# Attention scores of eight-wide heads in two 64-row tiles of TensorE, six bf16 products in place of nine, and their parts stored in stack order

## What is computed

```python
h = _layernorm(x) * (1 + ca) + sa
x = x + ga * attention_1(h)        # 16 heads of width 16, causal softmax
h = _layernorm(x) * (1 + cb) + sb
x = x + gb * ffn(h)
# ffn: layernorm, attention_2 (32 heads of width 8, full softmax), + input,
#      then per batch two of eight experts, 256 tokens each:
#      gelu(tokens @ w1 + b1) @ w2 + b2
```

## Time and profile before

| | us |
|---|---|
| median of three runs (1864.37 to 1867.82) | 1865.28 |
| span of the profiled execution | 1866.4 |
| TensorE matmuls busy | 1646.4 (88%) |
| VectorE busy | 1197.6 (64%) |
| ScalarE busy | 1020.4 (55%) |
| GpSimd busy | 479.6 (26%) |

### The profile page before, as it was taken

One profiled execution on the slowest core, in us unless ns is written; L12 is line 12 of the kernel. 1 busy time (PEld: TensorE's weight loads), 2 busy tenths in 40 slices (PEclk: granted clock), 3 DMA queues, 4 the chain that ended last, 5 costly groups with the idle time before them and its releaser, 6 DMA issues.

```text
span 1866.4 us, 32448 instructions
## 1 busy us (share of the span) xinstructions
PE 1646.4 (88%) x8721; PEld 717.9 (38%) x8721; DVE 1197.6 (64%) x3093; ACT 1020.4 (55%) x1967; POOL 479.6 (26%) x804
## 2 busy tenths in 40 slices
PE   3487769999899989999899989999899997989887
PEld 1223313336333543346333443335333452325325
DVE  7466367864787567864787557964687566665440
ACT  0044425765567555765467645765467654665561
POOL 7133312232232222331232221331231232200100
PEclk9789869999999999999899999999999999999898
DMA  4540162243443452243334342243324243132301
GB/s 113 124 96 20 55 134 62 61 93 82 114 92 81 84 130 55 61 99 81 103 81 95 78 130 62 69 94 87 103 72 95 73 100 72 35 63 68 97 2 57
DMA packets 92282, 152.61 MB, mean 82 GB/s; under 512 B 19748, under 2 KB 78180, under 8 KB 83820
## 3 DMA queue, kind: packets, MB, share of 16 engines
q1 hardware_dynamic: 92100, 150.40, 33.8%
HBM read 119.58 MB, written 29.59 MB: 80 GB/s over the span
## 4 chain that ended last, share of the span: by engine, by line
PE 67%; DVE 9%; DMA 7%; issue 6%; ACT 6%; SPq 3%; POOL 1%; DVEq 0%; POOLq 0%; ACTq 0%
PE bank_out L1058 14%; PE bank_scores L1042 13%; PE bank_max L1021 12%; PE bank_side L993 6%; PE bank_side L1148 5%; DMA q_stack<-max_parts 4%; PE bank_side L1006 3%; PE bank_misc L1132 3%; DVE neg_max L1250 3%; PE bank_side L1132 3%; ACT probs L855 2%; PE bank_side L1113 2%; SPq L646 2%; PE bank_misc L1067 2%; PE bank_misc L1103 1%
## 5 line engine op out<-in xcount | busy, mean ns | idle before, releaser
L855 ACT ACTIVATE probs<-bank_scores 128x512 f32<-128x512 f32 (+3 forms) x1536 | 790.4, 544 | 629.8 <-PE bank_scores L1042 624.9
L1250 DVE TENSOR_REDUCE neg_max<-bank_max 128x1 f32<-128x512 f32 x1024 | 668.7, 682 | 266.1 <-PE bank_max L1021 261.7
L1042 PE MATMUL bank_scores<-q_stack,k_stack 128*128 128x512 bf16 (+3 forms) x1536 | 555.2, 366 | 70.0 <-DMA q_stack<-max_parts 42.6
L1021 PE MATMUL bank_max<-k_stack,q_stack 125*128 125x512 bf16 (+3 forms) x1536 | 559.2, 372 | 58.7 <-issue 21.5
L1058 PE MATMUL bank_out<-probs,v_tile 128*9 128x512 f32 (+4 forms) x3072 | 367.6, 551 | 1.0 <-POOL probs L766 0.9
L1247 DVE CUSTOM_DVE_ANT_0 bank_max<-bank_max,causal 128x128 f32<-128x128 f32 (+3 forms) x512 | 247.4, 506 | 183.7 <-PE bank_max L1021 180.0
L1021 PEld LDWEIGHTS bank_max<-k_stack,q_stack 125*128 125x128 bf16 x1536 | 150.1, 99 | 441.3 <-issue 293.8
L1042 PEld LDWEIGHTS bank_scores<-q_stack,k_stack 128*128 128x128 bf16 x1536 | 151.4, 99 | 309.5 <-ACT probs L855 153.2
L748 POOL CAST max_parts<-max_row 16x128 bf16<-16x128 f32 x96 | 26.8, 279 | 593.7 <-DVE max_row L1261 593.4
L766 POOL TENSOR_SCALAR_AFFINE_SELECT probs<-probs 128x512 f32<-128x512 f32 x128 | 81.1, 634 | 343.4 <-ACT probs L855 343.4
L1148 PE MATMUL bank_side<-w_out,hidden_T 128*128 128x256 f32 x512 | 132.6, 386 | 13.7 <-ACT hidden_T L891 10.7
(11 more groups left out here) (115 smaller groups left out, 1388.1 us busy)
## 6 DMA issues: line engine op xcount, KB each, us to landing
q_stack<-q_parts SPq DMA_DIRECT2D x96, 192.0 KB
w_in<-in_L_ffn_w_dram SPq DMA_DIRECT2D x16, 1024.0 KB, 5.9
w_out<-in_L_ffn_w_dram SPq DMA_DIRECT2D x16, 1024.0 KB, 9.4
q_parts<-partsq SPq DMA_DIRECT2D x32, 384.0 KB, 2.6
k_parts<-partsk SPq DMA_DIRECT2D x32, 384.0 KB, 2.5
k_stack<-k_parts SPq DMA_DIRECT2D x96, 128.0 KB, 6.5
k_stack<-k_parts SPq DMA_DIRECT2D x32, 256.0 KB, 7.5
q_stack<-q_parts SPq DMA_DIRECT2D x16, 384.0 KB, 4.6
```

Source lines behind the costliest of these rows:

```text
L855: nc.scalar.activation(probs[s % 2][:, k, q0:S], region[bank][:, q0:S], ACT.Exp, scale=float(WIDTH[a]) ** -0.5).then_inc(drained[bank], 1)
L1021: pe.matmul(region[bank][:, 0:keys], q_stack[buf][0:r, hh, qt * P:(qt + 1) * P], k_stack[buf][0:r, hh, 0:keys], start=True, stop=True).the ...
L1042: pe.matmul(region[bank][:, q0:S], k_stack[buf][:, h, kt * P:(kt + 1) * P], q_stack[buf][:, h, q0:S], start=True, stop=True).then_inc(fill ...
L1250: v.tensor_reduce(dst, region[bank], AX_X, ALU.max).then_inc(drained[bank], 1)
```

## The change

For width 8 six products are kept (48 rows) in place of nine. A stack column now has two tiles of 64 rows: 48 rows of products, 13 of blanks and 3 of maxima, for two heads. Heads 0 and 1 of a group lie in rows 0 to 63, heads 2 and 3 in rows 64 to 127, and both matmuls of width 8 address 64 rows (the instruction streams from and writes to the same columns as before). The maxima of a slot are those of head (k + 2) mod 4, the scores those of head k, so the two are in different tiles. Width 16 keeps one tile of 128 rows; its maxima matmul has 128 rows too.

An item of the maxima is now a step (128 queries of four heads), for both attentions, `LEAD` is 8, and `max_rows` comes two steps after the last item of a group, which leaves it at the same step. In the causal attention all four maxima of a step have the same number of keys, and the step beside it has 512 - 128 * (s mod 4) score columns against 128 * (s mod 4 + 1) of maxima.

In DRAM the parts lie as eight slices in stack order; each piece is stored by three DMAs that repeat parts, twelve for an attention in place of four, and a stack is loaded by three DMAs (width 16) or four (width 8, in runs of two heads, 2 KB). The zero and one rows come from 18 DMAs at the start; POOL fills only a small block of ones and one of zeros. Weights are staged in `w_in` and `w_out`.

```diff
-LEAD = 7
+LEAD = 8
-Q_PARTS = ((0, 1, 2, 0, 1, 0), (0, 1, 2, 0, 1, 2, 0, 1, 2))
-K_PARTS = ((0, 0, 0, 1, 1, 2), (0, 1, 2, 1, 2, 0, 2, 0, 1))
+SLICES = 8
+FIRST_SLICES = ((0, 4, 6), (0, 3, 5))
+Q_COPIES = ((0, 3, False), (0, 2, False), (0, 1, False))
+K_COPIES = ((0, 3, True), (1, 2, True), (2, 1, True))
+BLANK_SLICES = ((3, 7), (6, 7))
+TILES = (1, 2)
+TILE_ROWS = (128, 64)
+MAX_ROW = 61
+ONES_DMAS = 18
+ROWS_AFTER = 2
+def tile_of(a, k):
+    return k * TILES[a] // GROUP
+def column_of(a, g, k):
+    per = GROUP // TILES[a]
+    return g % (UNIT_HEADS // GROUP) * per + k % per
+def turned(k):
+    return (k + GROUP // 2) % GROUP
...
-            waiting.setdefault((p + 1, ROWS_SLOT), []).append(("max_rows", ...
+            waiting.setdefault((p + ROWS_AFTER, ROWS_SLOT), []).append(("max_rows", ...
...
-    ahead = heads_of_attention(0, 0) + heads_of_attention(1, 0)
+    ahead = steps_of_attention(0, 0) + steps_of_attention(1, 0)
...
-                sp.dma_start(dst.rearrange("i p s -> p i s"), parts[t][:, :, oc, :]).then_inc(parts_stored[a], 16)
+                dst = dst.rearrange("i p s -> p i s")
+                for at, (part, n, again) in zip(FIRST_SLICES[a], (Q_COPIES, K_COPIES)[t], strict=True):
+                    src = parts[t][:, part:part + 1, oc, :].broadcast_to([P, n, S]) if again else parts[t][:, part:part + n, oc, :]
+                    sp.dma_start(dst[:, at:at + n, :], src).then_inc(parts_stored[a], 16)
...
-                    for g, part, n in runs(order):
-                        sp.dma_start(dst[g * d:(g + n) * d, :], src[part * d:(part + n) * d, :])\
-                          .then_inc(stack_loaded[u], 16)
+                    for t in range(TILES[a]):
+                        dst = stack[buf][t * TILE_ROWS[a]:(t + 1) * TILE_ROWS[a], 0:columns, :]
+                        dst = dst.rearrange("r (g k) s -> r g (k s)", k=per)
+                        for lo, hi in pieces:
+                            sp.dma_start(dst[lo:hi], src[t][lo:hi]).then_inc(stack_loaded[u], 16)
...
-                    dst = q_stack[buffer_of(u, b)][r + m:r + m + 1, h:h + GROUP, :].rearrange("p h (q t) -> p (h q) t", t=P)
+                    dst = q_stack[buffer_of(u, b)][MAX_ROW + m:P:TILE_ROWS[a], at:at + per, :]
...
-            pool.memset(k_stack[0][:, :, :], 1.0).then_inc(ones_made, 1)
-            for n in range(1, 3):
-                pool.memset(k_stack[n][:, :, :], 1.0).then_inc(ones_made, 1)
-            pool.wait_ge(ones_made, 3)
-            for n in range(3):
-                pool.memset(k_stack[n][0:P - M_PARTS, :, :], 0.0).then_inc(ones_made, 1)
-            pool.wait_ge(pro_drained, 9)
-            pool.wait_ge(perm_done, 4)
-            for n in range(3):
-                pool.memset(q_stack[n][:, :, :], 0.0).then_inc(ones_made, 1)
+            pool.memset(ones, 1.0).then_inc(ones_made, 1)
+            pool.memset(blank, 0.0).then_inc(ones_made, 1)
...
-                pe.matmul(region[bank][:, 0:keys], q_stack[buf][0:r, hh, qt * P:(qt + 1) * P],
-                          k_stack[buf][0:r, hh, 0:keys], start=True, stop=True).then_inc(filled[bank], 1)
+                kk = turned(k)
+                first, at = tile_of(a, kk) * TILE_ROWS[a], column_of(a, g, kk)
+                rows = slice(first, first + TILE_ROWS[a])
+                pe.matmul(region[bank][:, 0:keys], q_stack[buf][rows, at, qt * P:(qt + 1) * P],
+                          k_stack[buf][rows, at, 0:keys], start=True, stop=True).then_inc(filled[bank], 1)
...
-                pe.matmul(region[bank][:, q0:S], k_stack[buf][:, h, kt * P:(kt + 1) * P], q_stack[buf][:, h, q0:S],
+                first, at = tile_of(a, k) * TILE_ROWS[a], column_of(a, g, k)
+                rows = slice(first, first + TILE_ROWS[a])
+                pe.matmul(region[bank][:, q0:S], k_stack[buf][rows, at, kt * P:(kt + 1) * P], q_stack[buf][rows, at, q0:S],
                           start=True, stop=True).then_inc(filled[bank], 1)
```

More of the change, by code:

```diff
@@ L45 @@
 LN_PIECES = 5 + ROOT_STEPS
-def rows_of(a):
-    return WIDTH[a] * len(Q_PARTS[a])
-def runs(parts):
-    out = []
-    for g, part in enumerate(parts):
-        if out and part == out[-1][1] + out[-1][2]:
-            out[-1][2] += 1
-        else:
-            out.append([g, part, 1])
-    return out
+def tile_of(a, k):
[5 more added lines that the diff above has]
+    return (k + GROUP // 2) % GROUP
 PIECES = {"qk": 2, "v": 2, "attention_out": 2, "ffn_sum": 2, "expert_in": 2, "expert_out": 8}
@@ L117, in attention @@
         if p < len(lead) and lead[p][2] % GROUP == GROUP - 1:
-            waiting.setdefault((p + 1, ROWS_SLOT), []).append(("max_rows", lead[p][0], lead[p][1], lead[p][2] // GROUP))
+            waiting.setdefault((p + ROWS_AFTER, ROWS_SLOT), []).append(("max_rows", lead[p][0], lead[p][1], lead[p][2] // GROUP))
     for p, k in sorted(waiting):
@@ L143, in steps_of_attention @@
     return [(off, a, s) for s in range(T_STEPS * HEADS[a] // GROUP)]
-def heads_of_attention(off, a):
-    return [(off, a, h) for h in range(HEADS[a])]
 def layernorm_items(off, n):
@@ L228, in sections @@
     before += attention(steps_of_attention(0, 0) + steps_of_attention(1, 0), ahead[LEAD:], beside, hand_on=first)
-    first = [(at, (i[0], i[1] + 1, *i[2:])) for at, i in first]
-    before += attention([], heads_of_attention(0, 1)[:LEAD], {})
+    before += attention([], steps_of_attention(0, 1)[:LEAD], {}, hand_on=first)
+    first = sorted((at, (i[0], i[1] + 1, *i[2:])) for at, i in first)
     n1 = SLOTS * T_STEPS * HEADS[1] // GROUP
@@ L571, in unit_of @@
             return UNITS[a][h // UNIT_HEADS]
-        stack_dmas = [len(runs(Q_PARTS[a])) + len(runs(K_PARTS[a])) for a in (0, 0, 1, 1, 1, 1)]
-        for u in ZEROED_UNITS:
-            stack_dmas[u] += 1
+        stack_dmas = [1 + 2, 1 + 2, 2 + 2, 2 + 2, 2 + 2, 2 + 2]
+        copies = 4 * len(Q_COPIES)
         steps_of = [T * h // GROUP for h in HEADS]
@@ L680, in _ @@
                 sp.dma_start(st, w.rearrange("(c p) n -> p c n", p=P)).then_inc(weights_in, 16)
-            sp.wait_ge(ones_made, 4)
-            sp.dma_start(zero_dram[:, :], k_stack[0][0:PRODUCT_ROWS - rows_of(1), :, :].rearrange("p h s -> p (h s)"))\
-              .then_inc(mod_stored, 16)
+            sp.wait_ge(ones_made, 2)
+            for n in range(2):
+                src = blank[:, 0:2, :]
+                for i in range(2):
+                    for half in range(C):
+                        dst = q_dram[0][n, BLANK_SLICES[0][i], half * P:(half + 1) * P, :]
+                        sp.dma_start(dst, blank[:, 0, :]).then_inc(ones_in, 16)
+                for oc in range(C):
+                    dst = q_dram[1][n, oc, BLANK_SLICES[1][0]:SLICES].rearrange("i p s -> p i s")
+                    sp.dma_start(dst, blank[:, 0:2, :]).then_inc(ones_in, 16)
+            for n in range(3):
+                for t in range(TILES[1]):
+                    rows = slice((t + 1) * TILE_ROWS[1] - P // SLICES, (t + 1) * TILE_ROWS[1])
+                    sp.dma_start(k_stack[n][rows, :, :], ones.unsqueeze(1).broadcast_to([P // SLICES, UNIT_HEADS, S]))\
+                      .then_inc(ones_in, 16)
             sp.wait_ge(mod_rows_made, 6)
             sp.dma_start(mod_dram[:, :], mod_row[:, :, :].rearrange("b v d -> b (v d)")).then_inc(mod_stored, 16)
-            sp.wait_ge(mod_stored, 32)
-            sp.wait_ge(ones_made, 9)
+            sp.wait_ge(mod_stored, 16)
+            sp.wait_ge(pro_drained, 9)
+            sp.wait_ge(perm_done, 4)
+            sp.wait_ge(ones_in, 16 * ONES_DMAS)
             walk(sp, {"load_x": load_x, "load_residual": load_residual, "load_mod": load_mod, "load_gate": load_gate,
@@ L728, in qk @@
                     other, count = previous(a, b)
-                    wait_apart(pool, parts_stored[other], 64 * count)
+                    wait_apart(pool, parts_stored[other], 16 * copies * count)
                 pool.tensor_copy(parts[t][:, 1, oc, :], rest[:, buf, :]).then_inc(second_made[a], 1)
@@ L819, in qk @@
                     other, count = previous(a, b)
-                    wait(act, parts_stored[other], 64 * count)
+                    wait(act, parts_stored[other], 16 * copies * count)
                 nc.scalar.activation(parts[t][:, 0, oc, :], region[bank], ACT.Copy).then_inc(top_made[a], 1)
@@ L1011, in _, with maxima @@
             maxima_fill = {}
-            def maxima(b, turn, f, a, h, qt):
-                u = unit_of(a, h)
-                buf, hh, r = buffer_of(u, b), h % UNIT_HEADS, P - M_PARTS
-                if hh == 0 and qt == 0:
+            def maxima(b, turn, f, a, s, k):
+                g, qt = s // T, s % T
+                u = unit_of(a, g * GROUP)
+                buf = buffer_of(u, b)
+                if g * GROUP % UNIT_HEADS == 0 and qt == 0 and k == 0:
                     wait(pe, stack_loaded[u], 16 * stack_dmas[u] * (b + 1))
```

60 lines of the change are left out of this document (31 added, 29 removed).

## The result

The changed kernel takes **1881.87 us** (median of four runs, 1880.18 to 1884.22) beside 1866.48 for the kernel before (1864.37 to 1867.82): ratio 1.0082, interval 1.0068 to 1.0096. It is 0.8% slower, where the forecast was 1.5% faster. Its profiled execution took 1884.22 us, with a span of 1882.5; its TensorE clock is 0.949 on the mean, that of before 0.952.

A forecast was written before the change was run, and what follows sets the result against it. TensorE, 88% busy, was taken to bound most stretches. Tiles +21 in the loop and -9 after it, stacks -32 and -8, stores +1, lead +3, order +6, start -9 gave -27: 1838 us, range 1765 to 1905.

The forecast's parts named there:

- c: Price of each TensorE switch between 64-row and 128-row matmuls, taken as 0.10 us, bounds 0 and 0.16.
- switches' sum: Loop turn: 136 switches, 41 in pair steps with side work and 95 in mixed steps, cost 13.6 us a turn.
- The stalls: TensorE's waits at stacks: smaller loads save 32 us at stored maxima and 8 at two waits for a whole stack.
- The order of causal maxima: First attention: VectorE's maxima work becomes uneven between steps, costing 6 us, bounds 0 and 12.
- longer lead: Four more maxima before the first scores, where nothing else runs, cost 3 us net of a shorter tail.
- Pairs: Slots of pair steps: maxima and score take 0.22 us, not 0.44, saving 7.9 plus 2.2, 10.1 a turn.
- last section: After the loop, 56 pair steps and no mixed ones: pairs save 17 us, 80 switches cost 8; 9 saved.
- The start: Without POOL's large fills VectorE's first operations run sooner: 9 us saved, bounds 0 and 12.
- break-even: Whole kernel: the change neither gains nor loses if a switch costs 0.13 us, close to the assumed 0.10.
- rival of costlier switches: Switches at the 0.16 bound lengthen the mixed stretches, 30 and more us over the loop: 1891 us, chance 0.18.
- serial tiles: Pair slots: the two tiles don't run together, savings lost while switches stay: 1916 us, chance 0.14.
- free switches: Changes between 64 and 128 rows cost nothing or nearly: -117 us, 1748 us, chance 0.18.

The follow-up runs named there:

- run 2: Kernel before, width-8 maxima and scores both addressing rows 0 to 63 (one tile, switches without pairs): 2019.25 us over three executions, median with a fourth 2023.72, ratio 1.0829.
- run 4: Changed kernel with the causal maxima again taken head by head, as before the change: 1877.46 us, ratio 1.0038.
- run 8: Changed kernel with one 128-row tile, zeros loaded into the key stack's upper rows, and causal maxima head by head: 1838.90 us, ratio 0.9846.
- run 10: Changed kernel with one 128-row tile, zeros loaded, causal maxima head by head and a lead of 7: 1834.92 us, ratio 0.9825.
- run 1: Kernel before with only the tiles: width-8 maxima in rows 64 to 127, scores in rows 0 to 63: 1911.57 us, ratio 1.0218.
- run 3: Changed kernel without the tiles: width-8 matmuls address all 128 rows, adding up two heads in each score: 1819.79 us, ratio 0.9741.
- run 5: Changed kernel with the old lead, maxima seven steps ahead instead of eight: 1856.54 us, ratio 0.9947.
- run 6: Changed kernel reordered for half the switches, with matmuls of the same height beside each other and projection pieces together: 1840.85 us, ratio 0.9847.
- run 9: Changed kernel with causal maxima head by head, lead of seven and the order with half the switches together: 1825.52 us, ratio 0.9780.
- run 7: Changed kernel with one 128-row tile and zeros loaded into rows 64 to 111 of k, keeping the reference's output: 1842.94 us, ratio 0.9864.

## Why the prediction was wrong

**Right.** Tiles run together (starts 0.01 apart). c is 0.10 between bf16 matmuls, and the switches' sum of 13.6 us a turn is 13.9 in run 2, with 14 mixed steps for 16. It is right in part by accident: in the nine steps of run 2 there are 17 slots with 128-row work other than values behind a narrow score, not 22, but ten of them hold products alone, which pay the extra 0.10. 34 x 0.10 + 10 x 0.10 = 4.4; TensorE's busy time there grew by 46.31 - 41.98 = 4.33. The mixed stretches grew by 5.4 and 4.1 for "5 us each". ScalarE's pause fell to 0.70. The stalls shrank: 42.6 to 9.4 us for the stored maxima, where 32 was the term, and the two waits for a whole stack from 15.2 to 7.4 (4.79 and 2.58), where it was 8; a wait of 5.0 for the second stack of the run is new. The order of causal maxima cost 4 for 6 (runs 4, 8), the longer lead 4 for 3 where there are no tiles (run 10).

**The step that failed** is *Pairs*, "Nine steps with side work: 36 x 0.22 = 7.9 us", and with it the 10.1 a turn. Going from run 2 (switches, no pairs) to the changed kernel takes 46.31 - 39.38 = 6.9 us of work from TensorE in those nine steps, not far from 7.9. But the stretch shortens by only 46.55 - 42.40 = 4.15, and by the same in run 1 at full clock. The rest, 2.8 us, comes back as waits, nearly all for heads, act_T and neg_max of VectorE, in the rows shown. The prediction took a TensorE that is busy for 98% of a stretch as the bound by the full saving; it named VectorE as close behind only for the steps without side work. There 2.2 was forecast and 2.10 came (runs 1 and 2); in the changed kernel it is 1.46, since step 24, which the prediction counted among the ten pair steps, is a mixed one. So pairs bring some 6 us a turn, not 10.1. The switches of 16 mixed steps cost some 15, not 13.6. The turn's balance of tiles in these stretches is 9.9 (-0.49 - 0.42 + 5.74 + 0.85 + 4.19), not 3.5; the last 0.7 or so of the difference isn't split.

**In the last section** a net saving of 9 was forecast, from the shares of a turn. Behind the five turns the changed kernel takes 323.6 us, and run 3 without tiles 323.6 as well (1814.7 less 1283.18 less 207.92): these two traces show no saving. Their clocks differ there, 0.95 and 0.97 on the mean, so up to some 6 us of it may be hidden (an estimate: 2% of the section, at half of full speed, is 13 us at the lower level).

**Two smaller parts.** The back edge has no line in the sum. It costs 5.93 us on the mean where it cost 4.30, and it is 5.2 to 5.9 in all runs with 64-row matmuls (1, 2, 4, 5, 6, 9) and 4.3 to 4.5 in those without (3, 7, 8, 10); with tiles it is longer by about a microsecond, and no run says why. The 0.85 in the fourth stretch (36.41 to 37.26) is step 40, mixed through the longer lead: it isn't there in runs 1 and 2 (35.91, as before), whose lead is 7. The 9.9 (this 0.85 is in it) and the 1.65 of the back edge are 11.5; the first steps give 0.8 of it back, which makes the 10.7 a turn between the changed kernel and run 3.

**The start** was right at its place and wrong at its end. The first copy of wq runs at 18.79 where it ran at 25.26, and the modulation rows are there at 32.26 where they were at 40.27, 8 us earlier, for a term of 9 (DVE timeline):

```profile
18.79 1.02 DVE L1337 COPY wq<-bank_max 128x256 f32<-128x256 f32 x2 [7.88 <-PE bank_max L939]
...
32.26 0.17 DVE L1232 COPY mod_cur<-mod_T 128x4 f32<-128x4 f32 x1
```

The last one is 1.83 in the earlier trace rows, and the operation on hidden_T that took 2.23 there takes 0.41: beside POOL's fills they were stretched (the last three fills run from 31.39 to 42.08, and the copy of mod_cur ends at 42.10). "SBUF — State Buffer" of the Trainium skill, SBUF: two separate sides, has one port pair shared by VectorE and GpSimd, which, for the VectorE operations that need it, one of the two holds for a whole instruction; these rows agree. But only 3.6 us are left at the first causal maxima (81.84 to 78.27), since TensorE's first three groups of projections took 3.78 us each (PE timeline, the first):

```profile
36.34 3.78 PE L1014 MATMUL bank_side<-wv,act_T 128*128 128x256 f32 x8 [0.90 <-DVE act_T L1237]
```

Before, they took 3.52, 1.99 and 1.98; in run 3, with the same start, 3.45, 1.99 and 1.99. The second and third ran at the lower level here (granted clock 0.50 from 36.34 to 49.05; 1.00 before, from 49.30 to 53.96). It isn't the change's own: of runs 3 to 10, which have this start too, six have the first causal maxima at 74.7 to 75.8 (run 3: 75.49, 6.3 us earlier than before) and two at 78.6 and 78.9.

**The sum by its terms.** Tiles: +12 forecast (21 - 9), +62 measured (medians of the changed kernel and run 3). Of the 50 between them, the pairs are some 24 over six turns, the two mixed steps more some 8 to 10, the back edge 10, and the last section up to 9 (estimates from the figures above). All else: -39 forecast, -49 measured; what is found for its terms above comes to about -40 (33, 8 and 6.3, less 4 and 4), and the other 9 isn't split. The forecast sum of -27 became +15 (medians): the tiles alone turn the sign.

**The break-even** of c = 0.13 was the wrong number to hang the sign on. c came out at 0.10, and the kernel is slower: the other factor, what pairs save in a turn, was taken as known. The rival of costlier switches ("a weight load can't run ahead over a switch: fp32 side work loads 128 columns") came nearest by its mechanism and its time of 1891: the weight load does stand behind the switch and the extra 0.10 is there, but only for products behind 64-row matmuls, and the two mixed stretches that the rival named are no longer than c = 0.10 makes them. That its time is near is luck. The rivals of serial tiles and of free switches fell.

## What to carry to other kernels

Two half-height tiles at once halve the time of a pair (0.22 us for 0.44), but each piece of full-height work between two of them pays about 0.2 us for the trip, and an fp32 product 0.3: count the changes of shape in TensorE's order first, and put matmuls of one shape beside each other (run 6: 41 us). A stretch in which an engine is busy for 98% may give back only part of what is taken from it (here 4.15 of 6.9 us); before counting it, list which results of the next engine arrive just in time, since they become the new waits. And split a change with several parts: here the loads and the order of the stacks were worth 49 us, and the tiles, after which the change is named, cost 62.

## What was not expected of the hardware

The extra 0.10 us of an fp32 product of 128 columns behind a 64-row matmul, which one behind a 128-row matmul doesn't pay (1.06 and 0.96 to the next 64-row matmul). The back edge of the loop, longer with tiles (5.93 us on the mean beside 4.28 without). And the clock at the start of a turn: 0.77 in steps 0 to 3 of the changed kernel, where the stall is gone, beside 0.88 before; TensorE had stood still for 7.09 us ahead of them, beside 4.45. Behind the stall the kernel before had a second fall, which the changed one hasn't (1.00 from 705.04 on), as the prediction's signs had it:

```profile
701.42:710.09 8.67, 8.40 (x28) 2.55 (x28) 4.68 (x14) 4.66 (x8) 0.98 (x3) 0.68 0.00 0
```
